# Cross-attention on keys: a second score product with the largest taken off, in place of transposed probabilities

## The reference, cut to what matters

```python
qp = q @ Wq.T                                  # q = layernorm(x), 512 wide
k, v = jnp.split(latent_kv @ Wkv_expand.T, 2, axis=-1)
# 16 heads of 32: qh, kh, vh
scores = jnp.einsum('bhqd,bhkd->bhqk', qh, kh) * inv_sqrt_d
scores = jnp.where(causal, scores, jnp.finfo(scores.dtype).min)
attn = jax.nn.softmax(scores, axis=-1)
out = jnp.einsum('bhqk,bhkd->bhqd', attn, vh)
return out.transpose(0, 2, 1, 3).reshape(b, sq, H) @ Wout.T
```

## Time and profile before

| | |
|---|---|
| runs | 2691.79, 2698.35, 2704.05 us |
| the profiled execution's own time | 2698.37 us |
| its span, first to last instruction | 2696.6 us |
| PE busy | 2500.0 us (93%) |
| DVE, ACT, POOL busy | 66%, 43%, 32% |
| mean granted clock of PE | 0.971 |

### The profile page before, as it was taken

How to read it: one execution, slowest core, us unless ns; L and a number is a source line. 1 busy time by engine, 2 the same in 40 slices (tenths; PEclk the granted TensorE clock), 3 DMA queues, 4 the chain that set the end, 5 groups by cost and what they waited for, 6 DMA issues and landing times.

```text
span 2696.6 us, 46484 instructions
## 1 busy us (share of the span) xinstructions
PE 2500.0 (93%) x16390; PEld 1343.9 (50%) x16390; DVE 1791.3 (66%) x4037; ACT 1169.1 (43%) x2370; POOL 873.1 (32%) x801
## 2 busy tenths in 40 slices
PE   6999999999998999999768989989989989989998
PEld 3445454454544454444344454455455455455466
DVE  7789766777776777777475665665665665565554
ACT  4444444444444444444244534533543443543523
POOL 2333333333333333333123322422422422422413
PEclk9999999999999999999868999999999999999999
DMA  5677666776666677696420001001001001000000
GB/s 149 143 170 184 136 155 151 168 163 139 158 159 138 155 153 177 151 196 135 130 78 16 10 8 36 5 12 36 1 16 36 1 17 36 1 17 24 4 19 7
DMA packets 454606, 235.14 MB, mean 87 GB/s; under 512 B 388328, under 2 KB 391016, under 8 KB 454376
## 3 DMA queue, kind: packets, MB, share of 16 engines
q1 hardware_dynamic: 454376, 232.07, 36.5%
HBM read 78.66 MB, written 32.77 MB: 41 GB/s over the span
## 4 chain that ended last, share of the span: by engine, by line
PE 71%; DVE 13%; SPq 5%; issue 4%; DMA 3%; ACT 3%; POOL 2%; DVEq 0%; ACTq 0%; POOLq 0%
PE ps L1363 19%; PE ps L1364 19%; PE ps L1365 18%; DMA mem<-mem 3%; SPq L537 3%; DVE mem L1197 2%; PE ps L1496 2%; PE ps L1497 2%; PE ps L1498 2%; DVE mem L1201 2%; SPq L556 1%; PE ps L1506 1%; PE ps L1510 1%; PE ps L1508 1%; PE ps L1549 1%
## 5 line engine op out<-in xcount | busy, mean ns | idle before, releaser
L1363 PE MATMUL ps<-mem 128*128 128x512 f16 (+6 forms) x3924 | 1216.9, 329 | 93.7 <-DMA mem<-mem 39.1
L1364 PE MATMUL ps<-mem 128*128 128x512 f16 (+6 forms) x3924 | 1222.8, 328 | 0.0
L1365 PE MATMUL ps<-mem 128*128 128x512 f16 (+6 forms) x3924 | 1212.3, 327 | 0.0
L1363 PEld LDWEIGHTS ps<-mem 128*128 128x128 f16 (+3 forms) x3924 | 410.2, 105 | 420.4 <-issue 113.5
L1365 PEld LDWEIGHTS ps<-mem 128*128 128x128 f16 (+3 forms) x3924 | 411.1, 105 | 316.6 <-issue 17.1
L1364 PEld LDWEIGHTS ps<-mem 128*128 128x128 f16 (+3 forms) x3924 | 413.1, 105 | 303.5 <-issue 16.6
L697 POOL TENSOR_TENSOR mem<-mem 128x500 f32<-128x500 f32 (+1 forms) x231 | 270.4, 1170 | 359.3 <-ACT mem L928 198.9
L647 POOL TENSOR_TENSOR mem<-mem 128x8 f32<-128x8 f32 x100 | 163.7, 1637 | 541.8 <-DVE mem L1000 541.8
L1319 DVE TENSOR_TENSOR mem<-mem 128x500 f16<-128x500 f32 (+1 forms) x231 | 144.3, 648 | 189.9 <-ACT mem L910 186.2
L659 POOL TENSOR_TENSOR mem<-mem 100x400 f16<-100x400 f32 x128 | 162.2, 1267 | 187.7 <-ACT mem L799 187.7
L711 POOL TENSOR_TENSOR mem<-mem 100x400 f32<-100x400 f32 x128 | 107.9, 854 | 339.4 <-DVE mem L1211 339.4
(11 more groups left out here) (122 smaller groups left out, 3196.8 us busy)
## 6 DMA issues: line engine op xcount, KB each, us to landing
x<-mem SPq DMA_DIRECT2D x100, 256.0 KB, 3.0
mem<-x SPq DMA_DIRECT2D x75, 256.0 KB, 3.5
mem<-in_x SPq DMA_DIRECT2D x50, 256.0 KB, 3.7
mem<-x SPq DMA_DIRECT2D x12, 1000.0 KB
mem<-mem SPq DMA_DIRECT2D x32, 200.0 KB
out<-mem SPq DMA_DIRECT2D x6, 1000.0 KB
mem<-in_wq SPq DMA_DIRECT2D x4, 1024.0 KB, 5.7
mem<-in_wk SPq DMA_DIRECT2D x4, 1024.0 KB, 6.9
```

The lines of the kernel that those rows point to most:

```text
L1363: pe.matmul(out_ap, ah, bh, start=(i == 0), stop=False)
L1364: pe.matmul(out_ap, ah, bl, start=False, stop=False)
L1365: mm = pe.matmul(out_ap, al, bh, start=False, stop=(i == len(pairs) - 1))
```

## The change

The probabilities are formed with keys on the partitions, where the product with the values needs them, so that they are not transposed.

- PE forms the scores twice. The first time as before, for the largest of each query and head (DVE, `largest_scores`). DVE splits those 16 numbers a query into two bf16 parts, PE transposes them (`largest`, 100x128), DVE copies them to bf16 (`take_largest`). Then PE forms the scores with keys on the partitions and takes the largest off by a product with a matrix of minus ones (`shifted_scores`); ACT's exp reads them from PSUM.
- POOL puts zeros in for the causal mask (`affine_select`) in place of its multiplication.
- The sums come from PE: a product with a matrix of ones, in bank 5, beside the one with the values in bank 6. DVE inverts the 128x400 tile of sums and multiplies (`divide`); ACT and DVE split the product from SBUF.
- ACT's order in a batch: the weight splits of group 0, the copy of the result of b-1, then the four exps of b. DVE's: four largest, split, copy, `divide(b-1)`, `add_out`, `take_o(b-1)`, weight splits.
- PE's: scores of b, `mix(b-1)`, pieces, transpose of the largest, a piece, shifted scores, pieces. Output tiles alternate between banks 7 and 4, four pieces lie ahead of the first scores; the pieces need only the sum of the low-rank part (`dsum`) to start. The expert factors' banks 4 and 5 change places.
- POOL builds the ones, the zeros and the minus ones again in each group (three memsets, eight dependent `affine_select`), and its loop over the groups is written out.

```diff
-        OUT_AT, OUT_AFTER = {}, (6, 6)
-            OUT_AT[nb] = [[0, 0, 0, 0, 6 * n]] + [[n, n, n, n, 2 * n]] * (nb - 1) + [[n, n, n, 0, 3 * n]]
+        OUT_FIRST, OUT_AT, OUT_AFTER = 4, {}, {}
+        OUT_AT[GB] = [[4, 1, 3]] + [[3, 1, 3]] * (GB - 2) + [[3, 1, 0]]
+        OUT_AT[REST] = [[8, 2, 5]] + [[6, 1, 5]] * (REST - 2) + [[8, 2, 0]]
...
# POOL
+                for i in range(8):
+                    pool.wait_ge(c["const"], g * 11 + 3 + i)
+                    pool.affine_select(out=minus[:, :, :], in_=minus[:, :, :],
...
-                        pool.wait_ge(c["rden"], g * 4 * GB + 4 * b + i + 1)
-                        pool.tensor_tensor(cprobs[0:S, i, :, :], cprobs[0:S, i, :, :],
-                                           crden[0:S, i, :].unsqueeze(2).to_broadcast([S, HG, S]),
-                                           ALU.mult).then_inc(c["norm"], 1)
+                        pool.wait_ge(c["exp"], g * 4 * GB + 4 * b + i + 1)
+                        pool.affine_select(out=cpT[0:S, i, :, :], in_=cpT[0:S, i, :, :],
+                                           compare_op=ALU.is_ge, fill=0.0, base=0,
...
# ACT
+                    if b:
+                        act.wait_ge(c["pv"], g * GB + b)
+                        take_o(b - 1)
+                    for i in range(4):
+                        act.wait_ge(c["st"], g * 4 * GB + 4 * b + i + 1)
+                        act.activation(cpT[0:S, i, :, :],
+                                       ps[0:S, i, 0:HG * S].rearrange("p (h t) -> p h t", h=HG),
+                                       ACT.Exp).then_inc(c["exp"], 1)
+                take_o(nb - 1)
...
# DVE
+                def divide(b):
+                    dve.wait_ge(c["pv"], g * GB + b + 1)
...
+                    dve.reciprocal(cden_r[:, :, :],
+                                   ps[:, 5, 0:KC * S].rearrange("p (c t) -> p c t", c=KC)
+                                   ).then_inc(c["rden"], 1)
+                    dve.wait_ge(c["rden"], g * GB + b + 1)
+                    dve.tensor_tensor(co[:, :, :],
+                                      ps[:, 6, 0:KC * S].rearrange("p (c t) -> p c t", c=KC),
+                                      cden_r[:, :, :], ALU.mult).then_inc(c["co"], 1)
...
+                for b in range(nb):
+                    for i in range(4):
+                        largest_scores(b, i)
+                    split_largest(b)
+                    take_largest(b)
+                    if b:
+                        divide(b - 1)
+                    some_out(b)
                     if b:
                         take_o(b - 1)
...
# PE
+                def shifted_scores(b):
+                    pe.wait_ge(c["mxe"], g * GB + b + 1)
+                    for m in range(KC):
+                        for i in range(4):
+                            r0 = i * CD
+                            pe.matmul(ps[0:S, i, m * S:(m + 1) * S],
+                                      ckT[r0:r0 + CD, m, b * S:(b + 1) * S],
+                                      qpT[r0:r0 + CD, m, b * S:(b + 1) * S],
+                                      start=True, stop=False)
+                        for i in range(4):
+                            r0 = i * CD
+                            mm = pe.matmul(ps[0:S, i, m * S:(m + 1) * S],
+                                           minus[r0:r0 + CD, m, :], mxT[r0:r0 + CD, :],
+                                           start=False, stop=True)
...
+                for b in range(nb):
+                    scores(b)
                     if b:
-                        mix(b)
-                    some_out(OUT_AT[nb][b][4])
+                        mix(b - 1)
+                    some_out(OUT_AT[nb][b][0])
+                    largest(b)
+                    some_out(OUT_AT[nb][b][1])
+                    shifted_scores(b)
+                    some_out(OUT_AT[nb][b][2])
                 for t in early[:2]:
+                    project(t)
+                mix(nb - 1)
+                for t in early[2:]:
+                    project(t)
+                turn_row(g * 2 * NT + nt, nrm, 0, tm, 0)
...
```

More of the change, by code:

```diff
@@ L723, in _ @@
             cross_attention(0, GB, 0)
-            over_groups(pool, layer)
+            for g in range(FULL):
+                layer(g, GB, GB if g < FULL - 1 else REST)
+            if REST:
+                layer(FULL, REST, 0)
         @block.scalar
@@ L865, in cross_attention, with take_o @@
                                    ).then_inc(c["qpe"], 1)
[L867 to L881, removed]
+                def take_o(b):
+                    act.wait_ge(c["co"], g * GB + b + 1)
+                    act.activation(coT_hi[:, :, b * S:(b + 1) * S], co[:, :, :],
+                                   ACT.Copy).then_inc(c["ohi"], 1)
+                for b in range(nb):
                     for n in (beside_first(b) if not last_nb else []):
@@ L1205, in sum_probs @@
[L1205 to L1211, removed]
                 def add_residual(t):
@@ L1489, in project_out @@
                 if piece == 0:
+                    pe.wait_ge(c["dsum"], g + 1)
+                if piece == FC:
                     pe.wait_ge(c["dlo"], g + 1)
-                elif j == 0:
-                    pe.wait_ge(c["add"], g * NT + t)
+                if j == 0 and t >= 2:
+                    pe.wait_ge(c["add"], g * NT + t - 1)
                 h_hi, h_lo, w_hi, w_lo = ((hb_hi[:, j, a:b], hb_lo[:, j, a:b], wd_hi[:, j, :],
@@ L1559, in cross_attention, with scores @@
                 pe.wait_ge(c["qpe"], g * KC + KC)
+                def scores(b):
+                    for i in range(4):
+                        if b:
+                            pe.wait_ge(c["exp"], g * 4 * GB + 4 * (b - 1) + i + 1)
+                        pe.matmul(ps[0:S, i, 0:HG * S], ident16[0:S, 0:S],
+                                  mask[0:S, :, :].rearrange("p h k -> p (h k)"),
+                                  start=True, stop=False)
[5 more added lines that the diff above has]
+                                           ckT[r0:r0 + CD, m, b * S:(b + 1) * S],
+                                           start=False, stop=(m == KC - 1))
+                            if m == KC - 1:
+                                mm.then_inc(c["sc"], 1)
@@ L1567, in mix @@
                             h = 4 * m + i
[L1568 to L1569 removed]
+                            pe.matmul(ps[i * CD:(i + 1) * CD, 6, m * S:(m + 1) * S],
+                                      cv[0:S, b, h * CD:(h + 1) * CD], cpT[0:S, i, m, :],
+                                      start=True, stop=True)
+                    for m in range(KC):
+                        for i in range(4):
+                            mm = pe.matmul(ps[i * CD:(i + 1) * CD, 5, m * S:(m + 1) * S],
+                                           ones[0:S, :], cpT[0:S, i, m, :],
                                            start=True, stop=True)
[L1571 to L1572 removed]
+                    mm.then_inc(c["pv"], 1)
                 def project(t):
+                    pe.wait_ge(c["exp"], g * 4 * GB + 4 * (nb - 1) + t + 1)
                     pe.wait_ge(c["olo"], g * GB + -(-(t + 1) * tm // S))
```

193 lines of the change are left out of this document (99 added, 94 removed).

## The result

The kernel after took 2750.57 us (median of 4 runs, 2749.5 to 2751.76), beside 2696.93 us before: a ratio of 1.0195, 95% interval [1.0173, 1.0216]. It is slower by some 54 us; 2736 was forecast, with 2685 to 2768 as the range.

A forecast was written before the change was run, and what follows sets the result against it. The stage was taken as PE-bound with a 1.36 us wait a batch, the reciprocal's loop setting it after the change; 30 (five stages) + 6 (group 6) + 2 (group 0) = +38 on 2698.4, 2736 us, range 2685 to 2768.

The forecast's parts named there:

- The reciprocal's price: DVE's inversion of the 128x400 tile of sums, once a batch: 6 ns an element, 2.6 us.
- rival A: The wide reciprocal runs as other DVE operations do, 0.58 us; PE sets the batch, 2682 us in all; chance 0.18.
- The loop: Chain through DVE's reciprocal, ACT's copy and exps to PE's masks: 10.85 us a batch against 9.3 of PE issue.
- PE's added work: Second scores, sums, maxima transpose and bf16 products less the removed transposes: +0.85 us a batch, +4.2 a group of five.
- Rival B: Quick reciprocal, but alternating f32 and bf16 costs PE 0.45 us a batch: 2696; chance 0.10, shared with a 1-2 us reciprocal.
- The tail: End of a full stage: first output projection waits 2.8 us for the exps, fourth 2.3 us for the last division.
- The full stages: Cross-attention stages of groups 1 to 5: 67.5 us issue plus 10.7 idle, 78.2 against 72.2; five times gives +30.
- the term that I had put at nothing: PE's clock falls to the 1.2 GHz level in the five stages as waits grow, adding over 100 us; chance 0.04.
- Group 6: Cross-attention stage of the last two batches: 46.9 us issue plus 8.2 of waits, 55.1 against 48.6, +6.
- Group 0: First cross-attention stage, without output pieces, bound by the DVE and ACT chain: +2 us, between -3 and +6.
- the step that POOL's selects stay hidden within 0.2 us: POOL's four selects a batch, 0.547 us each, lie hidden under the spacing of ACT's exps within 0.2 us.
- Rival C: The wide reciprocal takes 3.4 us, lengthening three batches and two tail waits of each group: 2762 us; chance 0.13.

The follow-up runs named there:

- the run with that order alone: Kernel after with only ACT's order changed: the four exps of batch b ahead of the copy of b-1's result; 2709.01 us, 1.0041 of before.
- the run with all orders changed: Kernel after with exps first on ACT, pieces behind the last shifted scores, last value product ahead of projections, its division first in DVE's tail; 2682.21 us, 0.9946 of before.

## Why the prediction was right, and where it was off

- **The reciprocal's price.** Worked out from two and four elements, 6 ns an element and 2.6 us in all; measured 2.65 us, 32 times. This step carried the sign. It was a long one: the two shapes differ by 12 ns, and half a nanosecond of rounding in each would have moved the result between some 2.4 and 2.8 us. With the 0.58 us of other operations the kernel would have been faster than before (2678.9; rival A gave 2682).
- **The loop.** 10.85 us foreseen, 10.70 measured; mask waits of 0.8 and then spread masks, as foreseen (0.62 in the modelled ends, which is 0.8 in starts). That the copy ahead of the exps is the link is shown by the run with that order alone.
- **PE's added work.** +0.85 us a batch foreseen. Values and sums took 1.53 instead of 1.66, the shifted scores 1.20 instead of 1.34 (the bf16 products about 0.3, not 0.45); the output pieces and the steps between them took 0.17 more than foreseen, so that a middle batch that waits for nothing takes 9.20 us, beside 9.3 in the sum. The stage without the wide reciprocal was 69.5 in rival A and 68.4 measured. Rival B is out: no added price for the change between f32 and bf16.
- **The tail.** 2.8 and 2.3 us foreseen; 2.71 and 2.14 modelled, or 2.9 and 2.3 in starts.
- **The full stages** are 78.7 and 80.4 against 78.2. A stage without a fall of the clock would be about 77.1 (78.7 less the 1.6 of one drop), so the sum of work and waits was 1.1 too dear, and the clock made up for it and more: the term that I had put at nothing, a short fall of the clock in one or two places of each stage, was worth about 2 us. That 78.7 lies so near to 78.2 is luck in this part. Over five stages the sum was 30 foreseen, 36 measured.
- **Why the clock stood at nothing.** The prediction took the digit 9 of the page's clock row as a sign that the clock held behind group 6's wait of 2.61 us in the kernel before. A digit stands for 67 us and for anything from about 0.90 up. The trace of the kernel before has the fall there: the stretch from 2617.9 to 2689.9 has a clock of 0.93, and behind that wait the matmuls take 0.37 us for some 3 us before they take 0.25:

```profile
2626.89 0.37 PE L1365 MATMUL ps<-mem 128*128 128x200 f16 x1
...
2629.05 0.25 PE L1365 MATMUL ps<-mem 128*128 128x200 f16 x1
```

- **Group 6**: +6 foreseen, +8.4 measured, at a clock of 0.94 where I had reckoned with 1.00. Its three waits are 2.36, 1.68 and 3.88 us, where 2.4, 1.8 and 4.0 stood, so what is missing is the clock (PE is busy for 49.08 us, and for 46.72 in the run with all orders changed, at 1.00). **Group 0**: +2 foreseen, +6.0 measured, at the upper end of my bounds. There the step that POOL's selects stay hidden within 0.2 us failed: PE waits 3.6 us for them. The full stages give 5.8, group 6 some 2 and group 0 some 4 of the 14.6 us by which 2736 was low; the rest is within what the untouched part differs by between executions.
- **Rival C** (2762), with a reciprocal of 3.4 us, is out: it took 2.65. The Trainium skill ("VectorE: DVE Perf Modes", the walkthrough of the 8-slice pipeline) speaks of a repeat count of 8 for it; read as eight clocks an element, that is longer than what was measured, and the measurement decides.

## What to carry to other kernels

Before making an operation a hundred times wider, take its rate from two narrow shapes of its own in the trace, not from its neighbours: a reciprocal of four numbers hides a cost of 6 ns an element. A slow operation in a chain costs by who queues behind those that wait for it; the same reciprocal cost some 70 us here (2750.57 against 2678.9 without it), and once the exps stood ahead of the copy that needed it and pieces of other work lay over the tail, a full stage took 68.9 us with it, beside 68.4 in the run that left it out. If a stage is bound by such a wait, adding or removing work on the busiest engine tells little; change the order first, and then count the work. And a clock that looks full in a row of 40 slices may still fall for some us behind a wait: look at the durations of the matmuls behind it.

## What the runs showed of the hardware

- VectorE's reciprocal: 2.65 us for 128x400 f32 from PSUM, against 0.58 us for a product of that shape; halving its columns brought most full stages from 78.7 or 80.4 to 72.1 us.
- The granted clock falls behind waits that are short beside the stage. In the kernel after, with waits of 2.71 and 2.14 us ahead of the first and the fourth projection, it fell to the 1.2 GHz level once or twice a stage (0.98 and 0.96 on average); with waits of 3.31 us in three batches and longer ones ahead of two projections it was 0.85; with a single wait of 1.77 us it stayed at 1.00. With a wait of 2.14 us and none longer it was 1.00 in one stage and 0.98 in another. In the run with the doubled reciprocal the time of the stage grew faster than the chain: by 23.3 us, where the five added reciprocals account for 13.3.
- POOL's select of 100x400 took some 0.5 us an operation in f32 (four in 2.03 us), as it had in bf16 (0.55). Beside DVE's weight splits four took 6.13 us.
- Four copies of 125x512 f32 on DVE took 1.44 us alone and 4.83 beside POOL's product of 125x2048 (3.66 us), in the run with half the reciprocal.
